# Attention over a 32x32 image in split float32: softmax halves handled two position tiles at a time, and other first loads

## The reference

```
h = group_norm(x)                      # 32 groups of 16 channels
q, k, v = wq h + bq, wk h + bk, wv h + bv
attn = softmax(q^T k / sqrt(512))      # 1024 x 1024
out = x + wo (v attn^T) + bo
```

## Time and profile before

| | |
|---|---|
| median of 3 runs | 1977.85 us (1977.03 to 1978.11) |
| profiled execution, its own time | 1976.81 us |
| its span | 1974.8 us |
| TensorE busy | 1966.2 us (100%) |
| VectorE busy | 1630.7 us (83%) |
| ScalarE busy | 998.1 us (51%) |
| GpSimd busy | 327.0 us (17%) |
| granted TensorE clock, mean | 0.999 |

### The profile page before, as it was taken

How to read it: one execution, slowest core, us unless ns; L and a number is a source line. 1 busy time by engine, 2 the same in 40 slices (tenths; PEclk the granted TensorE clock), 3 DMA queues, 4 the chain that set the end, 5 groups by cost and what they waited for, 6 DMA issues and landing times.

```text
span 1974.8 us, 29827 instructions
## 1 busy us (share of the span) xinstructions
PE 1966.2 (100%) x9924; PEld 1680.8 (85%) x9924; DVE 1630.7 (83%) x2285; ACT 998.1 (51%) x1528; POOL 327.0 (17%) x240
## 2 busy tenths in 40 slices
PE   9999999999999999999999999999999999999999
PEld 7888888888888888888888888888888888888887
DVE  8998896978969789696887969889698896978857
ACT  6474453645536464454644536446364553646443
POOL 2022120111202012020121201212011120212202
PEclk9999999999999999999999999999999999999999
DMA  7336252363414535054350533615236252363402
GB/s 250 128 150 171 76 148 96 149 170 127 114 77 155 164 149 139 31 173 146 149 159 32 173 125 149 170 66 151 102 149 170 108 124 87 150 169 149 92 31 43
DMA packets 55035, 254.66 MB, mean 129 GB/s; under 512 B 8160, under 2 KB 8160, under 8 KB 50400
## 3 DMA queue, kind: packets, MB, share of 16 engines
q1 hardware_dynamic: 36720, 221.01, 29.8%
q0 software_dynamic: 18288, 33.30, 10.8%
HBM read 213.39 MB, written 74.45 MB: 146 GB/s over the span
## 4 chain that ended last, share of the span: by engine, by line
PE 94%; DVE 0%; issue 0%; POOL 0%; ACT 0%; POOLq 0%
PE psum L419 32%; PE psum L420 31%; PE psum L421 31%; DVE red L1161 0%; DVE scores L1166 0%; POOL wide L394 0%; DVE scores L1152 0%; DVE scores L1351 0%; DVE scores L1220 0%; ACT room L730 0%; POOLq L393 0%; ACT scores L744 0%
## 5 line engine op out<-in xcount | busy, mean ns | idle before, releaser
L419 PE MATMUL psum<-big_hi 128*128 128x512 f32 x1056 | 412.0, 390 | 1.6 <-POOL big_lo L361 1.6
L420 PE MATMUL psum<-big_lo,big_hi 128*128 128x512 f32 x1056 | 411.6, 390 | 0.0
L421 PE MATMUL psum<-big_hi,big_lo 128*128 128x512 f32 x1056 | 411.4, 390 | 0.0
L419 PE MATMUL psum<-big_hi,h_hi 128*128 128x512 f32 x896 | 348.5, 389 | 0.0
L420 PE MATMUL psum<-big_lo,h_hi 128*128 128x512 f32 x896 | 348.5, 389 | 0.0
L421 PE MATMUL psum<-big_hi,h_lo 128*128 128x512 f32 x896 | 348.5, 389 | 0.0
L1152 DVE TENSOR_TENSOR scores<-psum,room 128x512 f32<-128x512 f32 x192 | 130.6, 689 | 199.6 <-ACT room L826 149.6
L826 ACT COPY room<-psum 128x512 f32<-128x512 f32 x192 | 113.1, 589 | 291.2 <-PE psum L421 291.2
L419 PE MATMUL psum<-w_split,h_hi 128*128 128x256 f32 x896 | 253.6, 283 | 0.3 <-ACT room L730 0.3
L420 PE MATMUL psum<-w_split,h_hi 128*128 128x256 f32 x896 | 253.6, 283 | 0.0
L421 PE MATMUL psum<-w_split,h_lo 128*128 128x256 f32 x896 | 253.6, 283 | 0.0
(11 more groups left out here) (134 smaller groups left out, 3445.3 us busy)
## 6 DMA issues: line engine op xcount, KB each, us to landing
w_split<-kept_t SPq DMA_DIRECT2D x15, 3584.0 KB, 11.8
w_split<-kept_v SPq DMA_DIRECT2D x15, 3584.0 KB, 11.3
room<-in_x SPq DMA_DIRECT2D x64, 512.0 KB, 3.5
out<-scores POOLq DMA_DIRECT2D x127, 256.0 KB, 6.8
room<-in_x SPq DMA_DIRECT2D x61, 256.0 KB, 5.7
red<-in_x SPq DMA_DIRECT2D x30, 256.0 KB, 3.7
wide<-in_x SPq DMA_DIRECT2D x30, 256.0 KB, 6.9
kept_t<-w_split SPq DMA_DIRECT2D x1, 3584.0 KB, 10.9
```

Source lines behind the costliest of these rows:

```text
L419: nc.tensor.matmul(o, a_hi, b_hi, start=start, stop=False, skip_group_check=True)
L420: nc.tensor.matmul(o, a_hi, b_lo, start=False, stop=False, skip_group_check=True)
L421: return nc.tensor.matmul(o, a_lo, b_hi, start=False, stop=stop, skip_group_check=True)
```

## The change

- In the second half, `high_p` and `low_p` become `high_pair` and `low_pair`: one cast and one subtraction of 128x1024 for two neighbouring position tiles. `high_pair(n)` waits until both tiles of the pair are free. TensorE waits for a pair where it waited for each tile. PARTS is 12 for an image (8 singles and 4 pairs) in place of 16.
- ScalarE's order: `next_full(0)` and `high_h(b + 1, 0)` come after the second pair, `high_h` 1 and 2 after the third, and the fourth pair last.
- wk, wq, wo, bq and bo are read so that partition p holds rows 4p to 4p + 3 (one stretch of memory per partition), where it held rows p, 128 + p, and so on. The sums over channels come out the same. The output's channels are then 4p + k, and the stores and the last add-in of x follow. gamma, beta, wv and x stay.
- wk and wq come in three transfers each (rows 0, 1, and 2 with 3), wo in one.
- gamma, beta and bo are issued by ScalarE behind the bias terms, no longer by SP.
- 8 filler matmuls in place of 12.

```diff
+    PARTS = NJ + NJ // 2
+    LOADS = (slice(0, 1), slice(1, 2), slice(2, KC))
...
-    out_d = out.rearrange("b (k p) h w -> b k p (h w)", p=P)
-    w_d = {n: a.rearrange("(k p) n -> p k n", p=P) for n, a in (("q", wq), ("k", wk), ("v", wv), ("o", wo))}
-    bq_d, *vec_d = [a.rearrange("(k p) -> p k", p=P) for a in (bq, gamma, beta, bo)]
+    x_rows, out_rows = (a.rearrange("b c h w -> b c (h w)") for a in (x, out))
+    rest_d, out_d = (a.rearrange("b (p k) h w -> b k p (h w)", k=KC) for a in (x, out))
+    w_d = {n: a.rearrange("(p k) n -> p k n", k=KC) for n, a in (("q", wq), ("k", wk), ("o", wo))}
+    wv_d = wv.rearrange("(k p) n -> p k n", p=P)
+    bq_d, bo_d = (a.rearrange("(p k) -> p k", k=KC) for a in (bq, bo))
+    vec_d = [a.rearrange("(k p) -> p k", p=P) for a in (gamma, beta)] + [bo_d]
...
-            for o in range(KC):
-                sp.dma_start(wk_raw[:, o, :], w_d["k"][:, o, :]).then_inc(wk_in[o], 16)
-                sp.dma_start(wq_raw[:, o, :], w_d["q"][:, o, :]).then_inc(wq_in[o], 16)
+            for n, rows in enumerate(LOADS):
+                sp.dma_start(wk_raw[:, rows, :], w_d["k"][:, rows, :]).then_inc(wk_in[n], 16)
+                sp.dma_start(wq_raw[:, rows, :], w_d["q"][:, rows, :]).then_inc(wq_in[n], 16)
...
+            sp.dma_start(wo_raw, w_d["o"]).then_inc(wo_in, 16)
             for o in range(KC):
-                sp.dma_start(wo_raw[:, o, :], w_d["o"][:, o, :]).then_inc(wo_in[o], 16)
-            for n, a in enumerate(vec_d):
-                sp.dma_start(vecs[:, n, :], a, allow_slow_non_contiguous=True).then_inc(vec_in, 16)
-            for o in range(KC):
-                sp.dma_start(wv_raw[:, o, :], w_d["v"][:, o, :]).then_inc(wv_in[o], 16)
+                sp.dma_start(wv_raw[:, o, :], wv_d[:, o, :]).then_inc(wv_in[o], 16)
...
-                sp.dma_start(out_d[b], x_d[b].rearrange("p k n -> k p n")).then_inc(rest_in, 16)
+                sp.dma_start(out_rows[b], x_rows[b]).then_inc(rest_in, 16)
...
-            for _ in range(12):
+            for _ in range(8):
...
-                    pe.wait_ge(p_split, count(b, 16, n + 1))
+                    pe.wait_ge(p_split, count(b, PARTS, n + 1))
...
-                            pe.wait_ge(p_split, count(b, 16, NJ + n + 1))
+                            pe.wait_ge(p_split, count(b, PARTS, NJ + n // 2 + 1))
...
                 nc.scalar.activation(bias_terms[o], wk_raw[:, o, :], ACT.Identity,
                                      scale=bq_s[:, o:o + 1]).then_inc(terms_set, 1)
+            for n, a in enumerate(vec_d):
+                act.dma_start(vecs[:, n, :], a, allow_slow_non_contiguous=True).then_inc(vec_in, 16)
...
+            def high_pair(b, n):
+                j = 2 * G_PAIRS[n]
+                act.wait_ge(exp_set, count(b, 8, 4 + n + 1))
+                if n < 3:
+                    act.wait_ge(p_used, count(b, NJ - 1, 2 * n + 2))
+                else:
                     act.wait_ge(o_summed, count(b, 8, KC))
-                nc.scalar.copy(p_hi[:, j, :], scores[:, half * NJ + j, :]).then_inc(p_high, 1)
+                nc.scalar.copy(p_hi[:, j:j + 2, :], scores[:, NJ + j:NJ + j + 2, :]).then_inc(p_high, 1)
...
-                for n in range(NJ):
-                    high_p(b, 1, n)
+                for n in range(4):
+                    high_pair(b, n)
+                    if more and n == 1:
+                        next_full(0)
+                        act.wait_ge(v_summed, count(b, 28, 28))
+                        high_h(b + 1, 0)
                     if more and n == 2:
-                        next_full(0)
-                    if more and 3 <= n < 6:
-                        act.wait_ge(v_summed, count(b, 28, 28))
-                        high_h(b + 1, n - 3)
+                        high_h(b + 1, 1)
+                        high_h(b + 1, 2)
...
+            def low_pair(b, n):
+                j = 2 * G_PAIRS[n]
+                dve.wait_ge(p_high, count(b, PARTS, NJ + n + 1))
+                nc.vector.tensor_tensor(p_lo[:, j:j + 2, :], scores[:, NJ + j:NJ + j + 2, :],
+                                        p_hi[:, j:j + 2, :].bitcast(F32), ALU.subtract).then_inc(p_split, 1)
...
-                for j in range(4):
-                    low_p(b, 1, j)
-                for n in range(4, NJ):
-                    low_p(b, 1, n)
+                for n in range(4):
+                    low_pair(b, n)
```

More of the change, by code:

```diff
@@ L217, in attention_program @@
         bq_in, vec_in, bv_in = sem("bq_in"), sem("vec_in"), sem("bv_in")
-        wo_in = [sem(f"wo_in{o}") for o in range(KC)]
+        wo_in = sem("wo_in")
         wv_in = [sem(f"wv_in{o}") for o in range(KC)]
-        wk_in = [sem(f"wk_in{o}") for o in range(KC)]
-        wq_in = [sem(f"wq_in{o}") for o in range(KC)]
+        wk_in = [sem(f"wk_in{n}") for n in range(len(LOADS))]
+        wq_in = [sem(f"wq_in{n}") for n in range(len(LOADS))]
         x0_in = [sem(f"x0_in{k}") for k in range(KC)]
@@ L337, in image @@
                     sp.wait_ge(h_split, count(b, 7, 7))
-                    sp.dma_start(rest, x_d[b][:, KC - 1, HALF:N]).then_inc(rest_held, 16)
+                    sp.dma_start(rest, rest_d[b, KC - 1, :, HALF:N]).then_inc(rest_held, 16)
                     sp.wait_ge(rest_in, count(b, 16, 16))
@@ L439, in _ @@
             pe.wait_ge(consts_set, 4)
-            for c in range(KC):
-                pe.wait_ge(wo_in[c], 16)
+            pe.wait_ge(wo_in, 16)
             for n in range(KC):
@@ L745, in exponentials, with high_p @@
                                      scale=SCALE).then_inc(exp_set, 1)
-            def high_p(b, half, n):
+            def high_p(b, n):
                 j = J_ORDER[n]
-                act.wait_ge(exp_set, count(b, 8, half * 4 + n // 2 + 1))
-                if half == 1 and n < NJ - 1:
-                    act.wait_ge(p_used, count(b, NJ - 1, n + 1))
-                elif half == 1:
+                act.wait_ge(exp_set, count(b, 8, n // 2 + 1))
+                nc.scalar.copy(p_hi[:, j, :], scores[:, j, :]).then_inc(p_high, 1)
+            def high_pair(b, n):
[4 more added lines that the diff above has]
+                else:
                     act.wait_ge(o_summed, count(b, 8, KC))
-                nc.scalar.copy(p_hi[:, j, :], scores[:, half * NJ + j, :]).then_inc(p_high, 1)
+                nc.scalar.copy(p_hi[:, j:j + 2, :], scores[:, NJ + j:NJ + j + 2, :]).then_inc(p_high, 1)
             def bias_output(b, n, last=False):
@@ L845, in image @@
                 high_v(b, "C12", 1)
-                high_p(b, 0, 0)
-                high_p(b, 0, 1)
+                high_p(b, 0)
+                high_p(b, 1)
                 high_v(b, "C22", 1)
@@ L850, in image @@
                 exponentials(b, 0, 3)
-                high_p(b, 0, 2)
+                high_p(b, 2)
                 high_v(b, "C21", 1)
-                high_p(b, 0, 3)
+                high_p(b, 3)
                 high_v(b, "C11", 0)
-                high_p(b, 0, 4)
+                high_p(b, 4)
                 high_v(b, "C11", 1)
                 for n in range(5, NJ):
-                    high_p(b, 0, n)
+                    high_p(b, n)
                 def next_full(k):
@@ L1168, in centre, with low_p @@
                                         ALU.subtract).then_inc(centred, 1)
-            def low_p(b, half, n):
+            def low_p(b, n):
                 j = J_ORDER[n]
-                dve.wait_ge(p_high, count(b, 16, half * NJ + n + 1))
-                nc.vector.tensor_tensor(p_lo[:, j, :], scores[:, half * NJ + j, :], p_hi[:, j, :].bitcast(F32),
+                dve.wait_ge(p_high, count(b, PARTS, n + 1))
+                nc.vector.tensor_tensor(p_lo[:, j, :], scores[:, j, :], p_hi[:, j, :].bitcast(F32),
                                         ALU.subtract).then_inc(p_split, 1)
+            def low_pair(b, n):
[3 more added lines that the diff above has]
+                                        p_hi[:, j:j + 2, :].bitcast(F32), ALU.subtract).then_inc(p_split, 1)
             def add_v(b, x, r):
@@ L1192, in add_up @@
             def add_up(b, half):
-                dve.wait_ge(p_split, count(b, 16, half * NJ + NJ))
+                dve.wait_ge(p_split, count(b, PARTS, (NJ, PARTS)[half]))
                 e = scores[:, half * NJ:(half + 1) * NJ, :]
@@ L1301, in image @@
                 add_v(b, "C21", 0)
-                low_p(b, 0, 0)
+                low_p(b, 0)
                 add_v(b, "C21", 1)
                 low_v(b, "C21", 0)
-                low_p(b, 0, 1)
+                low_p(b, 1)
                 low_v(b, "C22", 1)
@@ L1309, in image @@
                 add_v(b, "C11", 1)
-                low_p(b, 0, 2)
-                low_p(b, 0, 3)
+                low_p(b, 2)
+                low_p(b, 3)
                 low_v(b, "C11", 0)
```

6 lines of the change are left out of this document (3 added, 3 removed).

## The result

The changed kernel takes 1982.12 us (median of 18 runs, 1981.07 to 1983.14); the kernel before took 1977.84 us in as many runs beside it. The ratio is 1.0023 with a 95% interval of 1.0017 to 1.003: 4.3 us slower, outside the predicted range and some 3 us beyond the forecast. The profiled execution took 1982.43 us with a span of 1980.8, so its span is 6.0 us longer than the one before. What lies around the span shrank from 2.0 to 1.7 us (mean of the runs).

The account below looks back on a forecast made before the run. TensorE, busy for 1966.2 of 1974.8 us, was taken to bound the kernel. Start -0.4 and loop +1.5 us made +1.1 on 1977.85: 1979.0 us for the median, range 1976.0 to 1981.5.

Parts of the forecast that it names:

- The passage between images: Pairs in the second half make h_lo, the snapshot copy and its weight load 0.10 us later, 15 times: +1.5 us.
- one for one rate: At the weight load behind copy L715: beyond 0.11 us of lead, each further delay costs the same amount of TensorE time.
- these four make up the rest of 7.09 us, 3.99: ScalarE, second half: one normalisation and three h_hi casts take 3.99 us, so the last pair can start at 257.19.
- upper bound of 3.0: Loop between images: if a 1024 pair is 0.1 us dearer, the loss is 0.20 x 15 = 3.0 us.
- the start's term: Before the first image: fewer fillers let the first product begin 1.3 us earlier, of which 0.4 us is taken as gain.
- all vectors must land by 21.4: Start: small vectors landing after 21.4 would hold up POOL's low_wv; costed at nothing, with +1 us as the end.
- middle of 0: Clock at the start: the slow stretch, 1.7 us lost, may vanish or double; taken as 0.
- the hole behind the fillers: Start: a 0.5 us hole between fillers and products may hold back the clock's first rise; 1.7 us either way.
- A: Rival: the loop between images loses nothing and only the start's gain is left, 1977.5 us; chance 0.25.
- B: Rival: all 1.3 us of the fillers, the slow clock stretch of 1.7 gone, no loop loss, 1974.9 us; chance 0.05.
- C: Rival: stores land late and VectorE's next-image sum L1032 waits; if landings double, 67 us, 2045; chance 0.04.
- D: Rival: a bigger stall at L715 or elsewhere in the pair's stage, from 0.35 us per image, 1982.7 us; chance 0.08.

Follow-up runs that it names:

- e4: The kernel before plus one clearing of an unread 128x256 tile on VectorE ahead of h_lo, a known delay; 1979.71 us, ratio 1.0016.
- e1: The kernel before with only the pairs, their order and PARTS; loads, layouts, fillers and stores as before; 1979.53 us, ratio 1.0013.
- e9: The kernel before with only wk, wq and bq laid out as rows 4p to 4p + 3 per partition; 1977.47 us, ratio 1.0007.
- e5: e2 with wk, wq and bq laid out as before, wo still in rows 4p; 1978.38 us, ratio 1.0006.
- e2: The changed kernel with the eight single casts of before; new loads, layouts, stores and 8 fillers stay; 1979.76 us, ratio 1.0014.
- e7: The kernel before with 8 filler matmuls for 12 and nothing else; 1977.36 us, ratio 1.0003.
- e12: The kernel before with gamma, beta and bo issued by ScalarE behind the bias terms; 1978.32 us, ratio 1.0008.
- e3: e1 with another ScalarE order: a pair between normalisation and first h cast, one h cast moved behind the last pair; 1976.49 us, ratio 0.9997.
- e6: e2 with four loads each for wk and wq, rows 4p + k kept; 1979.68 us, ratio 1.0013.
- e8: The changed kernel with e3's order, wk, wq and bq laid out as before, and four loads each for wk and wq; 1977.77 us, ratio 1.0002.
- e10: The changed kernel with only ScalarE's order changed to that of e3; 1978.91 us, ratio 1.0010.

## Why the prediction was wrong

**The passage between images: right place, wrong size.** The mechanism was forecast with its line and engine: weight loads that wait for the snapshot in every image, behind VectorE's h_lo, behind a pair that must be whole. VectorE's share was right to 0.01: from the start of the last pair to h_lo 2.22 us (262.43 - 260.21), forecast 1.05 + 0.03 + 1.13 = 2.21. The one for one rate was right, too (e4). The failed step is "these four make up the rest of 7.09 us, 3.99". That sum was carried over to an order in which the h cast stands directly behind the normalisation that it reads. They took 4.12: 6.97 us from the first to the last pair, less three casts of 0.95. With 2.22 for 2.21, h_lo was 0.24 late in place of 0.10, and the term 15 x 0.23 = +3.4 (e1 at one clock: +3.1 and +3.6) in place of +1.5. The upper bound of 3.0 was just short.

**The start: the failed step, by sign.** "The first low parts are ready at 4.85 + 0.69 = 5.54, so the first product can begin about 1.3 us earlier" took the time of the operands from before, although the rows of wk and wq had been moved in memory. The list of changes names the new layout of wk and wq, but the prediction's part on the start speaks only of bq's pieces and of wo's single transfer: the layout of wk and wq was costed at nothing, in silence. They landed late, the product began 0.57 later than before, and the start's term is +1.06 at wo\*wv in place of -0.4. One of the prediction's own signs of being wrong, wo\*wv after 23.8, came (24.85). e9 shows that the layout alone does it, e5 that the old layout wins two thirds of e2's delay back (1.04 of 1.55), and e7 that eight fillers alone would have given 0.7 at the first product and nothing at the end. That last point was half foreseen (the gain "doesn't reach the next stage whole"). Together the two terms make 1.06 + 3.4 = 4.5 us; the median rose by 4.3, with 0.35 less around the span.

**The small vectors.** Each issue took 0.44 to 0.54 on ScalarE, hidden as forecast, but not where it was forecast. They came at 11.50, 11.97 and 12.53, beside the last casts and the first bias terms (11.57, 12.09 and 12.61), which kept their usual step, and not in the idle stretch behind the bias terms. But "all vectors must land by 21.4" was named and then costed at nothing. In e12 the last lands at about 21.8. In the changed kernel the statistics are so late that it doesn't show.

**The clock.** The prediction's middle of 0 was not far off. The changed kernel's runs average a granted clock of 0.9985 against 0.9992. Were all of that lost TensorE time, it would be 0.0007 x 1980 = 1.4 us of the 4.3, but most of it is not. Part of the difference lies behind TensorE's last matmul, where a low clock costs nothing (profiled executions, before and after, last 4 us):

```profile
1970.70:1974.70 4.00, 0.00 (x0) 0.00 (x0) 1.44 (x2) 0.00 (x0) 0.00 (x0) 0.84 0.23 76
```

```profile
1976.70:1980.70 4.00, 0.00 (x0) 0.00 (x0) 1.44 (x2) 0.00 (x0) 0.00 (x0) 0.76 0.43 111
```

And the changed kernel's 9 runs at 0.998 have the same mean span as its 9 at 0.999, 1980.4. What is left: 24 of 99 runs of the kernel before are at 1.000 and 1.3 us shorter, and none of the changed kernel's 18: 24/99 x 1.3, an estimate of 0.3 us in the mean. Kernels with 12 fillers and SyncE's vectors (before, e1, e3, e4, e9) lie at 0.9992 to 0.9996, all those with 8 fillers or with the vectors moved at 0.9983 to 0.9990. That is a correlation over fourteen kernels and not shown as a cause: e7 and e12 differ from the kernel before by one edit each, and by 0.0002 and 0.0005.

What the prediction feared of the hole behind the fillers did come, though not in the changed kernel's profile: in those of e6, e8 and e10 the clock rose only 3.4 to 6.2 us into the products (last section). These three have 8 fillers, as have five kernels without it; none of the six with 12 shows it.

**The rivals.** A needed steps of 120.84; they are 121.08. B would have needed the 1.3 us of the fillers. C is out: the stores' median landing is 6.9 us against 6.8, and no engine waits for one. The Trainium skill's row on row distances (DMA: Bandwidth & Descriptors, "Latency and other measured facts") speaks of far larger ones, 512 KiB and up, which no run here has. D, a bigger stall at L715, is what came, at 0.23 an image and not 0.35. Its 1982.7 lies near the measured 1982.12 by luck: the start's loss, which D didn't have, fills the gap. The Trainium skill's rule that one large tile pays a latency once (VectorE: DVE Perf Modes, "The TRN2 errata — SBUF-src ops pay a fixed extra latency per instruction") holds here for the busy times, 11 us less on VectorE, and would have put the loop's term at 0. e3 shows the best that it gave: 0.

**What stays open.** e2 costs 2.1 us at one clock and 1.55 at wo\*wv. The layout alone (e9) costs 1.3 at one clock and 1.25 at wo\*wv; the rest fits the joint third transfers, for whose casts VectorE waits in e5, and the vectors, for which GpSimd waits in e8 and e12. Neither was tried alone on top of e5. Why the first image takes 121.3 us in one execution and 122.4 in another isn't known, nor why the clock rises late in some. No kernel here beats the one before beyond the uncertainty. e3's 0.9997 is the lowest, and at one clock it is no quicker.

## What to carry to other kernels

Merging two instructions saves their fixed cost only on an engine that isn't waiting. Where it waits for a producer, the merged one starts later, so count from the first input to the last consumer in the new order, and give an instruction directly behind its own producer the full duration of that producer. A new memory layout is a change to the arrival of every operand that it touches, even with the same bytes and the same issues: cost it at the first consumer of the first transfer. And before merging, delay the suspected instruction by a known 0.2 us (as e4 did); the step between images in its profile tells whether the place has any slack.

## What the runs showed of the hardware

- 128 rows of 2 KB that lie 8 KB apart come more slowly at the start than the same rows end to end: 224 and 113 GB/s against 293 and 198 from 2 to 6 us, the median landing of wk's four transfers 6.2 us against 4.6 (e9).
- An activation of 128x1024 gives ScalarE to the next instruction after 1.14 us; if the next reads its result, after 1.27 (all 14 times that the changed kernel's profile shows it). For ScalarE's own time that is small, and here it was 0.13 x 15 = 2 us of TensorE's.
- The same idle time of TensorE (1.65 us in the kernel before, 1.64 in e9) was followed by 3.4 us at the lower clock in one execution and by none in the other. The work ahead of it was the same but lay differently (the transposes at 19.06 and at 20.31), so the last idle time alone doesn't tell whether the clock falls.
- Behind the fillers the first products went 0.43 us apart for 3.1 us in e10's profile (idle 1.93 ahead of them) and 0.23 apart in the changed kernel's (idle 2.08). The view of stretches gives 1.00 for both, but in e10 that is no measurement: its trace has no record of the clock ahead of 10.72 us, which is where the step falls from 0.43 to 0.23. The fillers, ahead of any record, go 0.43 apart as well. So a granted clock of 1.00 in the first microseconds has to be checked against the matmuls' steps (e10):

```profile
9.99 0.63 PE L425 MATMUL psum<-big_hi 128*128 128x512 f32 x1
10.42 0.54 PE L426 MATMUL psum<-big_lo,big_hi 128*128 128x512 f32 x1
10.80 0.40 PE L427 MATMUL psum<-big_hi,big_lo 128*128 128x512 f32 x1
11.03 0.40 PE L425 MATMUL psum<-big_hi 128*128 128x512 f32 x1
```
